# Counting ties of the 32nd value, loading one stage earlier, and two pairs of heads in self attention

## What is computed

```python
# first layer, after cross attention and linear attention: eight experts
logits = einsum('bsd,ed->bse', x, gate_W) + gate_b
top1 = argmax(softmax(logits))
out = sum over i of (top1 == i) * (relu(x @ wi_W.T + wi_b + lora_i(x)) @ wo_W.T + wo_b)

# second layer: cross attention, each query keeps its 32 largest scores of 4096 keys
scores = einsum('bthd,bghd->bhtg', Q, K) / sqrt(32)
topv, topi = lax.top_k(scores, 32)
probs = softmax(topv)                         # all other keys get 0
attn_mean = mean of attn over the 4 heads     # then times V, FiLM, S4D, FFN, norms

# second layer: causal self attention, 16 heads of 16, rotary q and k
att = einsum('bhqd,bhkd->bhqk', q, k) / 4     # where causal, else -1e10
y = einsum('bhqk,bhkd->bhqd', softmax(att), v); out = y @ Wp + bp
```

## Time and profile before

| | us |
|---|---|
| median of 3 runs | 2199.34 |
| their range | 2195.12 to 2203.02 |
| the profiled execution's own time | 2203.82 |
| its span | 2202.0 |

### The profile page before, as it was taken

The page is one execution under the profiler, slowest core; times in us unless marked ns, Lnnn a source line. Parts: engine busy times, 40 slices in busy tenths (PEclk is TensorE's granted clock), DMA queues, the critical chain, the costliest instruction groups (busy, mean ns, idle before and its releaser), DMA issues. The chain is left out here.

```text
span 2202.0 us, 34851 instructions
## 1 busy us (share of the span) xinstructions
PE 1807.5 (82%) x13676; PEld 1104.1 (50%) x13676; DVE 1233.7 (56%) x3075; ACT 1025.5 (47%) x1381; POOL 759.8 (35%) x669
## 2 busy tenths in 40 slices
PE   5969999999999898888687877877766849888874
PEld 2434554454445444556466723544444437676653
DVE  5142424333332300364578379899999995557675
ACT  1457657756765687112131145555546521214442
POOL 6343324433542230000030027777878850110000
PEclk8989999999999999999967855878787669999897
DMA  6647555655756170000120001223132252000000
GB/s 143 118 105 127 117 109 109 117 119 113 122 109 128 56 125 38 1 2 1 58 70 1 14 1 44 79 59 87 51 86 66 58 184 86 1 1 1 1 6 15
DMA packets 78046, 150.01 MB, mean 68 GB/s; under 512 B 15464, under 2 KB 63144, under 8 KB 71464
## 3 DMA queue, kind: packets, MB, share of 16 engines
q1 hardware_dynamic: 64304, 101.80, 16.5%
q0 software_dynamic: 12768, 42.59, 12.7%
q10 hardware_dynamic: 792, 3.17, 0.4%
HBM read 93.59 MB, written 2.62 MB: 44 GB/s over the span
## 5 line engine op out<-in xcount | busy, mean ns | idle before, releaser
L571 ACT ACTIVATE P<-R 128x1024 f32<-128x1024 f32 x512 | 506.8, 1026 | 222.3 <-PE R L112 186.3
L112 PE MATMUL R<-QS,KST 100*128 100x256 bf16 x2048 | 297.0, 277 | 60.2 <-ACT P L571 53.5
L112 PEld LDWEIGHTS R<-QS,KST 100*128 100x128 bf16 x2048 | 170.0, 98 | 224.8 <-ACT P L571 120.9
L1797 POOL TENSOR_TENSOR ACC<-ACC,PM 128x4096 f32<-128x4096 f32 x22 | 195.2, 8872 | 1.8
L200 POOL TENSOR_TENSOR LNrs<-LNve,pk_const 128x2 f32<-128x2 f32 x36 | 25.3, 703 | 462.7 <-DVE LNve L196 462.5
L112 PE MATMUL R<-OV,QT 32*128 32x512 f32 x512 | 183.0, 802 | 0.0
L789 POOL DMA_DIRECT2D KST<-OV x300 | 144.5, 490 | 71.7 <-PE R L112 55.2
L112 PE MATMUL R<-P,VP 128*32 128x256 f32 x2304 | 156.1, 388 | 5.3 <-issue 5.0
L601 DVE CAST OV<-RT 128x512 bf16<-128x512 f32 x64 | 27.7, 432 | 217.2 <-ACT RT L116 130.0
L733 POOL CAST OV<-RT 128x512 bf16<-128x512 f32 x64 | 42.6, 665 | 266.5 <-DVE RT L604 266.5
L1787 POOL TENSOR_TENSOR SM<-SM,NG 128x1 f32<-128x1 f32 x30 | 79.3, 2644 | 147.5 <-DVE PM L1716 147.5
(11 more groups left out here) (370 smaller groups left out, 3559.0 us busy)
## 6 DMA issues: line engine op xcount, KB each, us to landing
KST<-OV POOLq DMA_DIRECT2D x276, 128.0 KB, 10.8
CT<-in_ctxP SPq DMA_DIRECT2D x40, 768.0 KB, 4.4
CN<-in_ctxn SPq DMA_DIRECT2D x60, 384.0 KB, 3.5
CT<-in_ctxT SPq DMA_DIRECT2D x64, 192.0 KB, 2.5
KST<-OV SPq DMA_DIRECT2D x84, 128.0 KB, 10.4
KST<-in_ctxP ACTq DMA_DIRECT2D x4, 768.0 KB, 9.4
QS<-x_q POOLq DMA_DIRECT2D x24, 128.0 KB, 5.4
pk_a<-in_pk_a SPq DMA_DIRECT2D x1, 3014.0 KB, 10.4
```

Source lines behind the costliest of these rows:

```text
L112: return e.matmul(o, l, r, start=st, stop=sp, skip_group_check=True)
L571: e.activation(P[(32 * p + k0) % 3][:, :], ring.at(("s", p, k0))[:, :], ACT.Exp).then_inc(*EX.up((p, k0)))
L1797: e.tensor_tensor(acc[:, :], acc[:, :], pm, ALU.add).then_inc(*G.up(("sum", p, h)))
```

## The change

It has three parts. In x1a, `top` makes three rounds in place of four, then one `tensor_scalar` over the 256 candidates with a sum: the 24 largest have been replaced by then, so it counts what is left at or above the 32nd value, eight if there is no tie. `scalar_tensor_tensor` adds that count to the flag, and `check` compares the sum of two heads and 128 rows with 2 * 128 * 8. In hla and moe, the loads of the packs s4d, x1a and moe and of the first key chunk are issued by SyncE in hla, into buffers of their own that live through both stages. In a1, `scores` is called twice for a unit, each for two heads with their masks, ahead of the product; the pieces q, k and ks come before `turn`, v after `weighted` and with ks' unit in place of k's. ScalarE makes both exponentials of a unit before the copies of the unit before it, and VectorE normalises unit u-1 between the two maxima of unit u.

```diff
+        def moe_loads(c, x1a):
+            t = {nm: pack(c, nm) for nm in ("moe", "s4d")}
+            keys = key_projection(c, x1a[1])
+            LW, W4 = dsig("w_moe"), dsig("w_s4d")
+            def sync(e):
+                load(e, "s4d", t["s4d"][0], W4)
+                load(e, "x1a", x1a[0], LA)
+                load(e, "moe", t["moe"][0], LW)
+                keys["sync"](e, 0, 0)
+            return dict(t, keys=keys, LW=LW, W4=W4, sync=sync)
...
             def sync(e):
-                load(e, "x1a", x1a[0], LA)
-                load(e, "moe", t_moe, LW)
-                load(e, "s4d", t_s4, W4)
                 for kind, *at in plan:
-                    if kind == "keys":
+                    if kind == "keys" and at[1] > 0:
...
-                    for r8 in range(4):
+                    for r8 in range(3):
                         if r8 > 0:
                             e.wait_ge(*V.now())
                         e.match_replace(CA[:, :], t8[:, 8 * r8:8 * r8 + 8], CA[:, :], SENT).then_inc(*V.up())
                         e.wait_ge(*V.now())
                         e.max(t8[:, 8 * r8 + 8:8 * r8 + 16], CA[:, :]).then_inc(*V.up())
                     e.wait_ge(*V.now())
-                    e.tensor_scalar(fl, fl, t8[:, 32:33], t8[:, 31:32], ALU.max, ALU.is_ge).then_inc(*V.up(("fl", p, h)))
+                    e.tensor_scalar(CA[:, :], CA[:, :], t8[:, 31:32], 0.0, ALU.is_ge, ALU.add, accum_out=t8[:, 32:33]).then_inc(*V.up())
+                    e.wait_ge(*V.now())
+                    e.scalar_tensor_tensor(fl, fl, t8[:, 31:32], t8[:, 32:33], ALU.is_ge, ALU.add).then_inc(*V.up(("fl", p, h)))
...
-                    with e.If_ne(reg["v"], 0):
+                    with e.If_ne(reg["v"], 2 * 128 * 8):
...
-                return [(b, p) for p in (("q",), ("k", "v"), ("ks",), ("norm", "xt"))[u % 4]] if b < NB else []
+                return [(b, p) for p in (("q",), ("k",), ("ks", "v"), ("norm", "xt"))[u % 4]] if b < NB else []
...
-                def scores(u):
+                def scores(u, g):
                     b, tl = u // 4, u % 4
                     QT, KT = buf("QT", b)[:, tl, :], buf("KT", b)[:, tl, :]
-                    if tl == 0:
+                    if tl + g == 0:
                         e.wait_ge(*V.at(("q", b)))
                         e.wait_ge(*V.at(("kt", b)))
-                    if u == 0:
+                    if u + g == 0:
                         e.wait_ge(*G.at("cm"))
-                    for j in range(4):
+                    if u > 0:
+                        e.wait_ge(*S.at(("ex", u - 1, g)))
+                    for j in (2 * g, 2 * g + 1):
                         rows = slice(32 * j, 32 * j + 32)
-                        if u > 0 and j % 2 == 0:
-                            e.wait_ge(*S.at(("ex", u - 1, j // 2)))
                         mm(e, SP4[j][:, 0:128], QT[rows, 0:128], KT[rows, 0:128], True, False)
-                    for j in range(4):
+                    for j in (2 * g, 2 * g + 1):
                         rows = slice(32 * j, 32 * j + 32)
                         mm(e, SP4[j][:, 128:384], QT[rows, 128:256], KT[rows, :], False, False)
-                    for j in range(4):
+                    for j in (2 * g, 2 * g + 1):
                         mm(e, SP4[j][:, 0:128], IDB[:, :], CMB[:, :], False, False)
                         ins = mm(e, SP4[j][:, 256:384], IDB[:, :], CMB[:, :], False, True)
-                        if j % 2 == 1:
-                            ins.then_inc(*M.up(("s", u, j // 2)))
+                    ins.then_inc(*M.up(("s", u, g)))
...
                 for u in range(NU + 1):
+                    if u < NU:
+                        scores(u, 0)
+                        scores(u, 1)
                     if product_at(u) is not None:
                         q_product(product_at(u))
-                    if u < NU:
-                        scores(u)
+                    for b, p in pieces(u):
+                        if p in ("q", "k", "ks"):
+                            piece(b, p)
                     if u > 0:
                         turn(u - 1)
                     for b, p in pieces(u):
-                        piece(b, p)
+                        if p == "xt":
+                            piece(b, p)
                     if u > 0:
                         weighted(u - 1)
+                    for b, p in pieces(u):
+                        if p == "v":
+                            piece(b, p)
...
-                    if u > 0:
-                        turned(u - 1, 0)
-                        turned(u - 1, 1)
                     if u < NU:
                         exp(u, 0)
+                        exp(u, 1)
                     if u > 0:
-                        turned(u - 1, 2)
-                    if u < NU:
-                        exp(u, 1)
+                        for n in range(3):
+                            turned(u - 1, n)
...
+                def maxima(u, g):
+                    if u >= 2:
+                        e.wait_ge(*S.at(("ex", u - 2, g)))
+                    ps = two(R[g][:, :])
+                    e.wait_ge(*M.at(("s", u, g)))
+                    for k in range(2):
+                        ins = e.tensor_reduce(buf("MX", u)[:, k, 2 * g:2 * g + 2], ps[:, :, parts[k]], AX.X, ALU.max, negate=True)
+                    ins.then_inc(*V.up(("mx", u, g)))
+                def normalise(u):
+                    e.wait_ge(*S.at(("ex", u, 1)))
+                    e.reciprocal(buf("SU", u)[:, :, :], buf("SU", u)[:, :, :]).then_inc(*V.up(("rc", u)))
+                    e.wait_ge(*V.at(("rc", u)))
+                    for k in range(2):
+                        part = buf("PS", u)[:, :, parts[k]]
+                        by = buf("SU", u)[:, k, :].rearrange("p (n o) -> p n o", o=1).broadcast_to(list(part.shape))
+                        e.tensor_tensor(part, part, by, ALU.mult).then_inc(*V.up(("sc", u, k)))
                 for u in range(NU + 1):
-                    for b, p in pieces(u - 1):
-                        if p != "norm":
-                            piece(b, p)
+                    if u < NU:
+                        maxima(u, 0)
+                    if u > 0:
+                        normalise(u - 1)
                     if u >= 6 and u % 4 == 2:
                         added(e, u // 4 - 1)
                     if product_at(u) is not None:
                         q_added(product_at(u))
+                    for b, p in pieces(u - 1):
+                        if p == "v":
+                            piece(b, p)
                     if u < NU:
-                        if u >= 2:
-                            e.wait_ge(*S.at(("ex", u - 2, 1)))
-                        for g in range(2):
-                            ps = two(R[g][:, :])
-                            e.wait_ge(*M.at(("s", u, g)))
-                            for k in range(2):
-                                ins = e.tensor_reduce(buf("MX", u)[:, k, 2 * g:2 * g + 2], ps[:, :, parts[k]], AX.X, ALU.max, negate=True)
-                            ins.then_inc(*V.up(("mx", u, g)))
+                        maxima(u, 1)
                         for job in quant(u):
                             quantise(*job)
                         for b, p in pieces(u + 1):
                             if p == "norm":
                                 piece(b, p)
-                        e.wait_ge(*S.at(("ex", u, 1)))
-                        e.reciprocal(buf("SU", u)[:, :, :], buf("SU", u)[:, :, :]).then_inc(*V.up(("rc", u)))
-                        e.wait_ge(*V.at(("rc", u)))
-                        for k in range(2):
-                            part = buf("PS", u)[:, :, parts[k]]
-                            by = buf("SU", u)[:, k, :].rearrange("p (n o) -> p n o", o=1).broadcast_to(list(part.shape))
-                            e.tensor_tensor(part, part, by, ALU.mult).then_inc(*V.up(("sc", u, k)))
+                        for b, p in pieces(u):
+                            if p in ("q", "k", "ks"):
+                                piece(b, p)
...
         KL = sbt(ctx, "KL", [128, 2, 256])
         x1a = pack(ctx, "x1a")
-        with ExitStack() as c:
-            stages.append(stage_moe(c, x1a))
+        with ExitStack() as both:
+            early = moe_loads(both, x1a)
+            with ExitStack() as c:
+                stages.append(stage_hla(c, early["sync"]))
+            with ExitStack() as c:
+                stages.append(stage_moe(c, early))
```

36 lines of the change are left out of this document (16 added, 20 removed).

## The result

| | before | changed |
|---|---|---|
| median, us | 2198.47 (2195.12 to 2203.02, 4 runs) | 2276.65 (2275.84 to 2281.46, 4 runs) |
| span of the profiled execution | 2202.0 | 2274.5 |
| mean granted clock of TensorE | 0.879 | 0.864 |

The ratio is 1.0359, 95% interval 1.0335 to 1.0383. The forecast was 2194, its range 2174 to 2212. So the kernel is 78 us slower than before, where I expected 5 faster, and both the sign and the range were wrong. The two profiled executions are 2274.5 - 2202.0 = 72.5 us apart, because the one of before lies above its own median.

What follows compares the result with a forecast made beforehand. VectorE was taken to bound x1a, a loop through three engines a1, and waits for loads to delay the experts' stage. 2203.8 (profiled) - 7.9 - 10.3 + 13.0 = 2198.6, less 4.5 to the median: 2194 us, range 2174 to 2212.

Steps and rivals of the forecast that it cites:

- The loads: Experts' stage: VectorE's 6.81 us wait for parameters goes, a later key chunk gives about 1 more; -7.9 us.
- The 3.5: Sign in the experts' stage: tables' setup begins about 3.5 us after the norms' start in place of 12.4.
- The ties: x1a: each `top` saves 0.54 us, 19 of 32 reach the stage's end; -10.3 us.
- the cost of the last operation: End of each `top` in x1a: 0.18 us in the new form, 0.27 before, for reading one fewer value.
- the count of 19: x1a: of 32 `top`s, 13 only lengthen VectorE's waits at boundaries and before the first data; 19 x 0.54 = 10.3 us.
- The loop of a light unit: a1, unit without projection: links through three engines sum to 9.5 us, 2.0 more than before, for fourteen units.
- C: Rival, a1: lower TensorE clock adds 2.0 us in each of seven light units, 14 in all; 2208, chance 0.30.
- the additions and the product in units 10 and 14: a1: product (1.97) and two additions come behind a projection's eviction; 2 x (1.97 + 1.3) + 0.5 = 7.0 us.
- The packs of two: a1: two score packs of two heads cost 2 x 0.87 us where one of four costs 0.87; 14 of TensorE time.
- the copies behind the eighth exponential: a1 light unit: three copies PT follow the second pair's exponentials in ScalarE's queue, 1.75 us of the loop.
- B: Rival, a1: pairs overlap, TensorE bounds the stage, 140 us in place of 157, a1 -12; 2169, chance 0.17.
- D: Rival, x1a: count not exactly 8, so all 16 pairs run the slow path, 1300 us more; chance 0.03.

Runs made afterwards that it cites:

- mended form: Changed kernel's count of ties, its last operation a tensor_scalar with two per-row scalars; alone against the kernel before 2189.66 us, ratio 0.9961.
- ties_no_second_tensor: Kernel before plus only the counting of ties, its last operation a tensor_scalar in place of scalar_tensor_tensor: 2189.66 us, ratio 0.9961.
- fitted filling: Kernel before with only a1's new order, plus unread TensorE products (5, 10 and 2) at three waits in units 3, 7, 11 to 16: 2223.33 us.
- a1_four_heads: Kernel before with only a1's new order, but the scores of a unit's four heads in one group as before: 2240.65 us.
- a1_both: Kernel before with a1's new order, but scores of four heads in one group and ScalarE's old order: 2237.10 us.
- a1_filler: Kernel before with only a1's new order, plus unread TensorE products (6, 16 and 5) at three waits in units 3, 7, 11 to 16: 2239.82 us.
- mended_with_filler: Kernel before with early loads, ties counted with a final tensor_scalar, a1's old order, eight unread products before the weighted sum of light units: 2186.45 us, ratio 0.9948.

## Why the prediction was wrong, step by step

**The loads: right.** -7.9 forecast, -8.8 in the profile and -9.3 alone. The tables' setup begins 5.4 us after the start of the norms, where before it was 12.3: the 6.8 that the sum had. The 3.5 that the prediction named as the sign was wrong, since the norms alone last 5.5 in the kernel before.

**The ties: the step that failed is the cost of the last operation.** The prediction took 0.18 us for it by the number of values it reads, and asked nothing about the other tensor or about GpSimd. It cost 2.63 on average, 77 us of waiting, and the stage became 47.8 longer where 10.3 less was forecast. The sign was there to see. In the earlier trace rows a GpSimd operation on one column takes 4.74 us; I used that row as a link of a chain and did not ask why one column takes that long. The same operation takes 0.54 to 0.59 where VectorE's select is not running. In the kernel before:

```profile
1309.08 4.48 DVE L1716 SCALAR_TENSOR_TENSOR PM<-S,T,PM 128x4096 f32<-128x4096 f32 x1
1309.24 4.72 POOL L1787 TENSOR_TENSOR SM<-SM,NG 128x1 f32<-128x1 f32 x1 [51.03 <-DVE PM L1716]
...
1317.72 0.56 POOL L1787 TENSOR_TENSOR SM<-SM,NG 128x1 f32<-128x1 f32 x1
```

15 of the 30 start 0.16 us after a select and end 0.40 after it; the other 15 meet none. So before the change the two engines already excluded each other, with GpSimd as the one who waited, and I put an operation of the excluded form on VectorE, in the stage in which VectorE is the bound. The rules of the Trainium skill, page SBUF — State Buffer, section SBUF: two separate sides, say so: the port pair that VectorE and GpSimd share is taken for a whole instruction, by a VectorE operation with two SBUF inputs against a GpSimd one that reads SBUF, and "the other fully blocks". By that rule the trace agrees, with 22 waits that end within 0.03 us of an addition's end, and with 0.27 us for the form with one tensor.

The other numbers of this part: the pass with a sum took 0.48 (taken 0.41), and with the mended form a `top` saves 0.47, not 0.54. 19 of 32 make 8.9, where the stage gained 2.8 to 3.0. The step that failed there is the count of 19. The sum let 13 `top`s be lost in longer waits at the boundaries, 13 x 0.54 = 7.0 us; but VectorE's idle time in x1a is 583.0 - 514.1 = 68.9 before and 580.2 - 510.9 = 69.3 in ties_no_second_tensor, and the account given there leaves 1.4 for the boundaries. What took the gain is a path that the sum did not have: inside the groups VectorE waits for GpSimd's additions, in the kernel before in five plain tensor_scalars, and what it saves ahead of such a place comes back as 5.8 + 4.7 us of longer waits. That is read from the durations; no run took these waits away.

**a1: the direction was right, the size was not.** Forecast +13, measured +40.3, of which +36.8 from unit 0 to 15 (194.1 against 157.3), where the sum had 168.6 + 0.9 = 169.5, or +12.2. Two terms failed and a third stays open.
- The loop of a light unit was 9.5; at full clock it is 9.8 to 9.9 (unit 12 with the fitted filling), in part by the third transposes that the sum left out. Over 14 units that is about 14 x 0.35 = 4.9.
- The clock was a rival, C, and not in the sum. It cost at least 13.2 us here, where the rival had 14. The rival had named seven light units at 2.0 us each; units 11 and 12 lost 24.5 - 20.1 = 4.4 and unit 8 lost 2.6, but unit 4 nothing, and 13 and 14, which it did not name, lost 2.8 and 1.9. To put this term at nothing in the sum was the larger error.
- The rest is 180.8 - 169.5 - 4.9 = 6.4, and it was not traced. It holds what the fitted filling itself costs and the clock that is still missing to 1 in that run.
- One term was right but for the clock, the additions and the product in units 10 and 14. They stand between the maxima: in unit 14 of the changed kernel the first maxima start at 2209.96 and the second at 2217.66, 7.7 apart, where a light unit has 2.9.

```profile
2209.96 1.02 DVE L2524 TENSOR_REDUCE MX<-R 128x2 f32<-128x256 f32 x2 [10.71 <-PE R L112]
...
2212.87 0.69 DVE L2569 TENSOR_TENSOR X<-B,X 128x512 f32<-128x512 f32 x1
2213.59 0.69 DVE L2571 TENSOR_TENSOR X<-X,pk_a 128x512 f32<-128x512 f32 x1
...
2213.61 3.40 PE L112 MATMUL B<-q_WT,q_XT 128*128 128x256 f32 x8 [2.57 <-DVE X L2569]
...
2217.06 0.69 DVE L2513 TENSOR_TENSOR X<-B,X 128x512 f32<-128x512 f32 x1 [2.77 <-PE B L112]
2217.66 1.01 DVE L2524 TENSOR_REDUCE MX<-R 128x2 f32<-128x256 f32 x2
```

The product waits for the first addition, the last addition for the product (3.40 at the low clock, 1.97 in the earlier trace rows), and the second maxima for that. Of the 4.8 that this adds, 1.4 is the low clock's, and the 3.4 left is what the sum had, 7.0 / 2 = 3.5.

I had also named the wrong culprits. The packs of two and the copies behind the eighth exponential stand in my walk of the loop, but a1_four_heads and a1_both show that, with the late normalisation kept, four heads in one group make the time 3 us longer and ScalarE's old order takes 3 off. Moving the normalisation alone makes 31 us from the old side and takes back 22 from the new one. The effects do not add, since with an early normalisation the new order is still 18 us above before; which of its other points makes that was not separated.

**The rivals.** B (overlap) did not happen. C did, on top of a longer loop. D was not the case: x1a has the same 32 selects and fewer operations of VectorE than before, not the slow path's passes over 4096 columns. None of the rivals was the mechanism that decided, the wait for GpSimd.

## What to carry to other kernels

Before an operation is put on VectorE beside a busy GpSimd, count its tensors in SBUF first, not its columns: a per-row scalar (tensor_scalar with two of them) did the same work in 0.27 us where a second one-column tensor cost 2.6. That holds for the form measured here, one column wide; plain tensor_scalars over 128 and 256 columns waited as well, with one tensor. If an operation of one column takes microseconds anywhere in a trace, look for a wait, and for the engine it waits for, before the first edit. Where an engine waits for another further down its queue, time saved ahead of that place can come back as waiting. And in a loop through several engines, ask of a moved step what stood beside it: the normalisation's 2 us cost 31 over 15 units because its successors lost their cover, and with the pauses that this made TensorE's clock was lower as well (0.80 in place of 0.91).

## What the runs showed of the hardware that was not expected

- A VectorE scalar_tensor_tensor with two SBUF tensors and a GpSimd tensor_tensor did not overlap: 128x1 takes up to 5.90 us behind an addition of 8.86. With the additions in four parts the longest is 1.71.
- Two tensors are not the only form that waits. A pair of plain tensor_scalars over 256 float32 columns (L1660) takes 0.73 us where GpSimd is idle; in the kernel before it took 1.90 and 2.00 during additions, and in ties_no_second_tensor 2.86, while an addition ran from 1382.54 to 1391.44. The one over 128 columns (L1667) did the same. The tensor_scalar with a sum and the one over a single column never did, 32 times each. The Trainium skill, page SBUF — State Buffer, section SBUF: two separate sides, counts an operation in a two-port performance mode among those that take the shared ports; which of these forms are in one, the runs don't show apart from this.
- A tensor_scalar over 256 float32 columns takes 0.48 with a sum; without one it takes 0.29 in the earlier trace rows, and 0.40 to 0.41 with two per-row scalars (L1660).
- Unread products on TensorE made a real stretch faster: clock 1.00 in place of 0.57, 20.1 us in place of 24.5. Where they did not fit the gap, they gave nothing in the time (a1_filler) or made units 0 to 15 3.5 us longer (mended_with_filler).
